# A TensorE that branches on each expert's token count, eleven more early casts, and a last norm shared by two engines

## The chip, the cores and the metric

The kernel is one launch on the 8 cores of a Trainium2 chip. Cores 0 to 3 are on one die, 4 to 7 on the other. No core waits for another, and each works on its own 1,024 tokens. The metric is the device time in microseconds of the slowest core.

## The reference

One transformer layer with the norms behind the residual sums. First attention over 4 sequences of 2,048 tokens (width 2,048, 16 causal heads of 128), then a norm; then a mixture of experts and another norm:

```python
h = relu(einsum('td,ndf->ntf', flat, shared_w1) + shared_b1)     # 2 shared experts, 1408 wide
out = flat + einsum('ntf,nfd->td', h, shared_w2) + shared_b2.sum(0)
scores = sigmoid(flat @ centroids.T) + bias                      # 16 routed experts
vals, idx = top_k(scores, 4)                                     # each token goes to 4 of them
gating = scattered vals / their sum
for each expert: rout += (relu(flat @ w1 + b1) @ w2 + b2) * g[:, None]
x = layernorm(x + out + rout)      # x is the input of this half
```

All inputs are float32; the kernel computes in bfloat16 with float32 sums. A core's 1,024 tokens times 4 choices over 16 experts make 256 tokens for an expert on average.

## The kernel before

**Stages.** Each core runs attention, then the output projection with the first norm (`wo_tile`, `ln1_tile`), then the router, then the 16 routed experts one after the other (the loop `for j in range(NR)`), and at the end the last group of the shared experts with the final norm (`dense_group(GROUPS[-1], ..., after_tile=final_norm)`).

**Two bodies.** After the router every engine reads a flag (L1254) and branches (L1255, L1257): the sparse body is run when no expert has more than CAP = 320 tokens, else a dense body that stands behind it in the instruction stream and is as long again.

**A routed expert (sparse body).** Its tokens are gathered by an indirect DMA (L1028) and turned by TensorE (`turn_batch`, L1043) into `xgT`, always 320 columns, with empty places where there are fewer tokens. The first product (L1127) takes 11 slices `fc` of 128 hidden units, 16 matmuls of 320 columns each; ScalarE applies the relu (L1134). The second product goes in two passes `h` over halves of the output: at each of 11 steps `fc`, four matmuls of 512 columns for the first two tiles of 128 tokens (L1154), and then two matmuls with 64 stationary columns (L1160) for the third tile, tokens 256 to 319. The results are written to `y_scr` by indirect DMAs (L1194). Between the steps `tick` spends a number of matmuls (`FILL_AT`) of the shared experts, which a generator hands out (L752, L774; DVE adds at L789).

**Weights.** They lie in HBM as float32 and are wanted as bfloat16 in units of 512 KB. A unit is either loaded by GpSimd's queue with a cast on the way (L687), or cast early from HBM to HBM into `wpre` by `precast` (L246) and later loaded as bfloat16 by SyncE's queue (L678). Experts 0, 2, 4, 6, 8, 10 and 14 (`PRE_EXPERTS`) are cast early, 22 units each; experts 1, 3, 5, 7, 9, 11, 12, 13 and 15 are cast at their load. The units go through a ring of 9 slots (two of them are held by the generator's group while it is open): `release` frees a slot when the last matmul that reads it is done, and `pump` then issues the next load in the order of use. The early casts are issued 6 after each load of attention's weights, `PRE_WO` = 16 after the loads of Wo, and the rest behind the loads of the first shared group. At most four are in flight (`DMA_POOLS["pre"]`), and GpSimd's queue waits in order.

**End.** `combine_load` and `combine_add` (L1091, L1096) add the experts' outputs. Then `final_norm` takes each of 8 token tiles: four bn_stats on VectorE (L572), a short chain of [128,1] operations (L580 to L586, with a Sqrt on ScalarE at L584), and two ScalarE passes that scale the tile (L807). VectorE's queue runs in program order, so the four additions of the next tile (L789) stand behind this tile's chain.

Of the kernel before, what the change touches and what calls it, by code (L numbers as in the profile page):

```python
# [15 lines left out]
D = 2048  # L16
# [6 lines left out]
FCH = 11  # L23
# [13 lines left out]
PRE_WO = 16  # L37
# [22 lines left out]
class SB:  # L60
# [50 lines left out]
    def mark(self, sem):  # L111
        return self.cnt.get(sem, 0)

# [21 lines left out]
def build_nc():  # L135
# [39 lines left out]
    sidx_sb = small("sidx_sb", 96, U32)  # L175
    flag_sb = small("flag_sb", 8, I32)
# [54 lines left out]
    sel_bf = carve(76800, 128)  # L231
    g_sb = carve(77056, 256, F32)
# [4 lines left out]
    def emit(plans):  # L237
# [353 lines left out]

        def wo_tile(n, ti, dns):
# [288 lines left out]
        flag_dv = sb.vchain(lambda e: e.tensor_scalar(flag_sb[:, 0:1], gsum[:, 8:9], CAP + 0.5, None, ALU.is_gt))  # L881
        sb.vchain(lambda e: e.tensor_scalar(pos, sel, -FAR, FAR - SHIFT, ALU.mult, ALU.add))
# [90 lines left out]
        IOA = bass.IndirectOffsetOnAxis  # L973
        limit_regs = {}
# [135 lines left out]
        for j in range(NR):  # L1110
# [29 lines left out]
            for h in range(2):  # L1140
# [7 lines left out]
                for fc in range(FCH):  # L1148
                    pu, po = divmod(h * FCH + fc, 2)
                    w = use(("w2", ge, pu))  # L1150
                    sb.wait("tensor", *hr_ready[fc])
                    for t in range(2):
                        for dn in range(2):
                            sb.mm((lambda e, fc=fc, w=w, po=po, t=t, dn=dn: e.matmul(  # L1154
                                psum_bank(2 * t + dn), Hr(fc)[:, t * 128:(t + 1) * 128],
                                w[:, po * 1024 + dn * 512: po * 1024 + (dn + 1) * 512],
                                start=(fc == 0), stop=(fc == FCH - 1), skip_group_check=True)), False)
                    end = fc == FCH - 1
                    for dn in range(2):
                        m = sb.mm((lambda e, fc=fc, w=w, po=po, dn=dn, end=end: e.matmul(  # L1160
                            PP[dn * 64:(dn + 1) * 64, 4 * 512:5 * 512], Hr(fc)[:, 256:CAP],
                            w[:, po * 1024 + dn * 512: po * 1024 + (dn + 1) * 512],
                            start=False, stop=end, skip_group_check=True)),
                            dn == 1 and (po == 1 or end))
                    if po == 1:
                        release(("w2", ge, pu), m)
                    if not end:
                        if j + 1 < NR and (h, fc) in TURN_AT:
                            turn_batch(j + 1, TURN_AT[h, fc])
                        tick(per)  # L1170
# [191 lines left out]
```

## Time and profile before

| | us |
|---|---|
| median of 3 runs (lowest, highest) | 2643.47 (2641.03, 2645.89) |
| the profiled execution, its own time | 2636.41 |
| its span on the slowest core (core 2) | 2634.7 |
| spans of the 8 cores | 2594.9 to 2634.7 |
| core 2: first matmul of expert 0 / of expert 15 / last matmul of expert 15 | 1258.1 / 2405.3 / about 2516 |
| PE busy, DMA share and granted clock over the span | 2296.7 (87%) / q0 73.9% and q1 15.6% / 0.945 |

The profiled execution's time is its span and 1.7 us around it, and lies 7 us below the median of the runs. A matmul's record is longer than the time until the next one can start, since they are pipelined, so rates are read from stretches of many. Rows name an engine, or its queue with a q behind it.

### The profile page before, as it was taken

The page shows a single profiled execution, that of the slowest core. Times are in us where ns is not written, and L with a number is a line of the kernel's source. Part 1 is how long each engine was busy: PE and PEld are TensorE (multiplying, and loading weights), DVE is VectorE, ACT ScalarE, POOL GpSimd, SP SyncE. Part 2 cuts the span into 40 slices and gives each one's busy share as a digit, 9 for nine tenths or more (in the row PEclk, how much of TensorE's full clock was granted, in tenths as well). Part 3 has the DMA queues.
Part 4 walks back from the last instruction along what each step waited for, and adds up shares of the span by engine and source line. Part 5 has one row for each costly group of instructions (what it writes and reads, how often), then busy time and mean ns, then how long its engine had stood idle before and what let it go on. Part 6 is the DMA issues. An engine that isn't in the chain of part 4 may idle for free.

```text
span 2634.7 us, 36044 instructions; the slowest of 8 cores (2594.9 to 2634.7 us)
## 1 busy us (share of the span) xinstructions
PE 2296.7 (87%) x13723; PEld 1200.7 (46%) x13723; DVE 865.8 (33%) x1397; ACT 544.2 (21%) x817; POOL 377.8 (14%) x583
## 2 busy tenths in 40 slices
PE   5879999999999569978989999899989988898776
PEld 3536646556466334423544444444534444244221
DVE  0234444444444334574201111113111031534356
ACT  0023333334334432201111111110101111011003
POOL 1001111111010000000021212122222212102100
PEclk9989999999999779999999999999999998999888
DMA  9499999999998895597499898989898999989973
GB/s 163 65 121 121 121 122 120 120 121 120 122 120 100 160 133 126 113 128 135 159 171 265 173 254 189 247 195 217 213 225 218 181 180 203 243 282 205 223 218 129
DMA packets 113360, 442.48 MB, mean 168 GB/s; under 512 B 16004, under 2 KB 16516, under 8 KB 103456
## 3 DMA queue, kind: packets, MB, share of 16 engines
q0 software_dynamic: 80208, 300.15, 73.9%
q1 hardware_dynamic: 32976, 139.94, 15.6%
q8 instruction: 116, 1.90, 0.3%
q14 instruction: 60, 0.49, 0.1%
HBM read 647.84 MB, written 139.46 MB: 299 GB/s over the span
## 4 chain that ended last, share of the span: by engine, by line
DMA 49%; PE 38%; DVE 6%; issue 4%; ACT 2%; POOL 1%; DVEq 0%; POOLq 0%; SPq 0%; ACTq 0%
DMA wpre<-w1x 12%; DMA wpre<-w2x 12%; DMA ar<-w2x 8%; PE PP L1154 8%; PE PP L1127 8%; DMA ar<-y_scr 6%; DMA ar<-w1x 5%; PE PP L774 4%; PE PP L598 3%; PE PP L1160 3%; PE PP L752 2%; PE PP L1043 2%; PE PP L322 2%; PE PP L341 2%; DVE ar L1096 1%
## 5 line engine op out<-in xcount | busy, mean ns | idle before, releaser
L1127 PE MATMUL PP<-ar 128*128 128x320 bf16 x2816 | 413.0, 305 | 44.0 <-DMA ar<-w1x 37.4
L1154 PE MATMUL PP<-ar 128*128 128x512 bf16 x1408 | 379.6, 394 | 17.5 <-DMA ar<-w2x 17.4
L1127 PEld LDWEIGHTS PP<-ar 128*128 128x128 bf16 x2816 | 276.4, 99 | 182.6 <-issue 64.2
L322 PE MATMUL PP<-ar 128*128 128x512 bf16 x1024 | 244.4, 382 | 29.4 <-DMA ar<-wqkv 29.3
L774 PE MATMUL PP<-ar 128*128 128x512 bf16 x704 | 208.4, 411 | 68.2 <-DVE ar L789 47.5
L477 ACT COPY ar<-PP 128x1024 bf16<-128x1024 bf16 (+1 forms) x192 | 153.3, 799 | 475.9 <-PE PP L466 475.9
L789 DVE SCALAR_TENSOR_TENSOR ar<-PP,ar 128x512 f32<-128x512 f32 x256 | 169.8, 688 | 218.8 <-PE PP L774 203.3
L341 PE MATMUL PP<-ar 128*128 128x256 bf16 x2048 | 241.5, 273 | 0.0
L1052 DVE COPY ar<-PP 128x960 bf16<-128x960 bf16 x96 | 55.9, 599 | 539.7 <-PE PP L1043 538.6
L436 DVE TENSOR_REDUCE st_sb<-PP 128x1 f32<-128x256 f32 (+7 forms) x128 | 173.7, 1357 | 171.7 <-PE PP L430 162.8
L341 PEld LDWEIGHTS PP<-ar 128*128 128x128 bf16 x2048 | 197.6, 98 | 30.3 <-issue 0.2
L1154 PEld LDWEIGHTS PP<-ar 128*128 128x128 bf16 x1408 | 124.7, 100 | 189.4 <-issue 76.9
L752 PE MATMUL PP<-ar 128*128 128x512 bf16 x704 | 174.0, 382 | 12.8 <-DVE ar L890 8.8
L1134 ACT ACTIVATE ar<-PP,b_sb 128x320 bf16<-128x320 f32 x176 | 92.8, 527 | 417.6 <-PE PP L1127 410.1
L306 PE MATMUL PP<-ar 128*128 128x512 bf16 (+1 forms) x576 | 130.5, 369 | 39.8 <-DMA ar<-xT 29.0
L1181 ACT COPY ar<-PP 128x512 f32<-128x512 f32 x64 | 34.4, 589 | 633.5 <-PE PP L1160 633.5
L322 PEld LDWEIGHTS PP<-ar 128*128 128x128 bf16 x1024 | 96.9, 98 | 134.2 <-issue 41.0
L446 ACT ACTIVATE ar<-PP,st_sb 128x256 bf16<-128x256 f32 (+7 forms) x128 | 156.9, 1226 | 0.5 <-DVE st_sb L436 0.5
L1160 PE MATMUL PP<-ar 128*64 128x512 bf16 x704 | 146.8, 414 | 0.0
L466 PE MATMUL PP<-cb_sb,ar 128*128 128x128 bf16 x1152 | 101.3, 227 | 37.5 <-ACT ar L477 32.5
L1096 DVE SCALAR_TENSOR_TENSOR ar<-ar,gk_sb 128x2048 f32<-128x2048 f32 x32 | 75.3, 2352 | 178.5 <-DMA ar<-y_scr 177.7
L687 POOL DMA_DIRECT2D ar<-w1x x117 | 65.1, 561 | 450.7 <-PE PP L1160 247.2
(117 smaller groups left out, 1858.7 us busy)
## 6 DMA issues: line engine op xcount, KB each, us to landing
ar<-wpre SPq DMA_DIRECT2D x162, 512.0 KB
ar<-w1x POOLq DMA_DIRECT2D x117, 512.0 KB, 14.1
ar<-w2x POOLq DMA_DIRECT2D x117, 512.0 KB, 19.1
wpre<-w1x POOLq DMA_DIRECT2D x81, 512.0 KB, 24.8
wpre<-w2x POOLq DMA_DIRECT2D x81, 512.0 KB, 24.8
ar<-y_scr SPq DMA_DIRECT2D x32, 1024.0 KB
ar<-wqkv POOLq DMA_DIRECT2D x24, 1024.0 KB, 25.1
ar<-xT POOLq DMA_DIRECT2D x8, 1024.0 KB, 27.1
```

The source lines that it names most:

```text
L306: (lambda e, dc=dc, rhs=rhs: e.matmul(ps[:, 0:w], w_at["q"][:, dc * 256 + jl * 128: dc * 256 + (jl + 1) * 128], rhs, start=(dc == 0), stop ...
L322: (lambda e, dc=dc: e.matmul(ps, w_at["k"][:, dc * 256 + jl * 128: dc * 256 + (jl + 1) * 128], x_bf[:, c * 8192 + dc * 512: c * 8192 + (dc ...
L341: (lambda e, dc=dc, tl=tl, sub=sub: e.matmul(ps[:, sub * 256:(sub + 1) * 256], x_bf[:, c * 8192 + dc * 512 + tl * 128: c * 8192 + dc * 512 ...
L436: sb.do("vector", lambda e: e.reduce_max(negmx_sp[up], PP[:, 0:kc], axis=AX.X, negate=True), "dv", 1)
L446: lambda e: e.activation(p_sb[up][:, 0:kc], PP[:, 0:kc], AF.Exp, bias=negmx_sp[up], scale=1.0, accum_out=lsum_sp[up]),
L477: lambda e: e.copy(dst, tb[:, 0:nbl * 128].rearrange("p (kb n) -> p kb n", n=128)), "ac", 1)
L752: m = sb.mm((lambda e, dc=dc, w=w, bank=bank, nt=nt: e.matmul(psum_bank(bank), w[:, dc * 128:(dc + 1) * 128], xhat[:, dc * 1024 + nt * 512 ...
L774: m = sb.mm((lambda e, j=j, w=w, bank=bank, ti=ti, dn=dn, last=last: e.matmul(psum_bank(bank), Hs[j][:, ti * 128:(ti + 1) * 128], w[:, dn ...
L789: x_mark[ti, dn] = sb.vec((lambda e, xs=xs, bank=bank, sc=sc: e.scalar_tensor_tensor(xs, psum_bank(bank), sc, xs, ALU.mult, ALU.add)))
L1127: m = sb.mm((lambda e, dc=dc, w=w, bank=bank: e.matmul(psum_bank(bank)[:, 0:CAP], w[:, dc * 128:(dc + 1) * 128], xgT[:, dc * CAP:(dc + 1) ...
L1154: sb.mm((lambda e, fc=fc, w=w, po=po, t=t, dn=dn: e.matmul(psum_bank(2 * t + dn), Hr(fc)[:, t * 128:(t + 1) * 128], w[:, po * 1024 + dn * ...
L1160: m = sb.mm((lambda e, fc=fc, w=w, po=po, dn=dn, end=end: e.matmul(PP[dn * 64:(dn + 1) * 64, 4 * 512:5 * 512], Hr(fc)[:, 256:CAP], w[:, po ...
```

## The change

Three edits. TensorE loads the 16 token counts into registers at the start of the sparse body. For each of the 11 slices of the first product it then has two versions of the 16 matmuls, one of 320 columns and one of 256, each under an If on the count. In the second product the third tile's matmuls are put ahead of the others, for two steps at a time (`PASS_STEPS`), under an If that leaves them out when the expert has at most 256 tokens. Eleven more units (the second product's weights of expert 12) are cast early, by `PRE_WO` = 27. In the final norm tiles 0, 2, 4 and 6 get their sums from two ScalarE passes with accumulation.

```diff
-PRE_WO = 16
+PRE_WO = 27
+PASS_STEPS = [[(0, 1), (2, 3), (4, 5), (6, 7), (8, 9), (10,)],
+              [(0,), (1, 2), (3, 4), (5, 6), (7, 8), (9, 10)]]
+PRE_HALF = 12
...
+    units += [("w2", 2 + PRE_HALF, u) for u in range(FCH)]
...
+        def act_scale(ti):
...
+            scr = final_scr
+            for dn in range(4):
+                sb.wait("scalar", *x_mark[ti, dn])
+            sb.act(lambda e: e.activation(scr, x_tm[ti], AF.Copy, bias=0.0, accum_out=ssum))
+            sb.wait("scalar", "ac")
+            m = sb.act(lambda e: e.activation(scr, x_tm[ti], AF.Square, accum_out=ssq))
+            sb.wait("vector", *m)
+            sb.vec(lambda e: e.tensor_scalar(mean, ssum, 1.0 / D, None, ALU.mult))
+            sb.vec(lambda e: e.tensor_scalar(r, ssq, 1.0 / D, EPS, ALU.mult, ALU.add))
+            sb.vchain(lambda e: e.scalar_tensor_tensor(bcol, mean, -1.0, mean, ALU.mult, ALU.mult))
+            sb.vchain(lambda e: e.tensor_tensor(r, r, bcol, ALU.add))
+            m = sb.vchain(lambda e: e.reciprocal(r, r))
...
         def final_norm(ti):
-            for chunk in range(4):
-                ln_stats(ti, chunk)
-            m, rinv, bcol, _, _ = ln_scale(ti, False)
+            if ti % 2:
+                for chunk in range(4):
+                    ln_stats(ti, chunk)
+                m, rinv, bcol, _, _ = ln_scale(ti, False)
+            else:
+                m, rinv, bcol = act_scale(ti)
...
+        cnt_dv = sb.vec(lambda e: e.tensor_scalar(cnt_sb[:, :], pbank[:, 128:144], 1.0, None, ALU.max))
...
+        sb.wait("tensor", *cnt_dv)
+        sb.take_counts("tensor")
...
-                for dc in range(16):
-                    sb.wait("tensor", *xgT_ready[j, dc // 3])
-                    m = sb.mm((lambda e, dc=dc, w=w, bank=bank: e.matmul(
-                        psum_bank(bank)[:, 0:CAP], w[:, dc * 128:(dc + 1) * 128], xgT[:, dc * CAP:(dc + 1) * CAP],
-                        start=(dc == 0), stop=(dc == 15), skip_group_check=True)), dc == 15)
+                for b in range(6):
+                    sb.wait("tensor", *xgT_ready[j, b])
+                m = sb.either("tensor", j, *[[(lambda e, dc=dc, w=w, bank=bank, cols=cols: e.matmul(
+                    psum_bank(bank)[:, 0:cols], w[:, dc * 128:(dc + 1) * 128], xgT[:, dc * CAP:dc * CAP + cols],
+                    start=(dc == 0), stop=(dc == 15), skip_group_check=True)) for dc in range(16)]
+                    for cols in (CAP, 256)])
...
-                for fc in range(FCH):
-                    pu, po = divmod(h * FCH + fc, 2)
+                for fcs in PASS_STEPS[h]:
+                    pu = (h * FCH + fcs[0]) // 2
                     w = use(("w2", ge, pu))
-                    sb.wait("tensor", *hr_ready[fc])
...
+                    for fc in fcs:
+                        sb.wait("tensor", *hr_ready[fc])
+                    sb.only_if("tensor", j, [(lambda e, fc=fc, w=w, po=(h * FCH + fc) % 2, dn=dn: e.matmul(
+                        PP[dn * 64:(dn + 1) * 64, 4 * 512:5 * 512], Hr(fc)[:, 256:CAP],
+                        w[:, po * 1024 + dn * 512: po * 1024 + (dn + 1) * 512],
+                        start=False, stop=(fc == FCH - 1), skip_group_check=True)) for fc in fcs for dn in range(2)])
...
+            if item[0] == "counts":
+                counts = [e.value_load(cnt_sb[0:1, i:i + 1]) for i in range(NR)]
+            elif item[0] == "if":
+                with e.If(counts[item[1]] > 256):
+                    for fn in item[2]:
+                        fn(e)
+            elif item[0] == "either":
+                with e.If(counts[item[1]] > 256):
+                    for fn in item[2][:-1]:
+                        fn(e)
+                    item[2][-1](e).then_inc(sems["pe"], 1)
+                with e.If(counts[item[1]] < 257):
+                    for fn in item[3][:-1]:
+                        fn(e)
+                    item[3][-1](e).then_inc(sems["pe"], 1)
```

The four L1154 matmuls of each step follow the If as before, and the slot is released behind them.

## Rows read from the trace of the kernel before

**Rows 1.** The cores: span from first to last instruction, mean granted clock.
```profile
core 0: 2632.3 us, clock 0.945
core 2: 2634.7 us, clock 0.945
core 7: 2630.7 us, clock 0.947
```

**Rows 2.** Core 2 by stretches, experts 0, 4, 5, 12: busy time (count), PEclk, DMA share, GB/s.
```profile
core 2: us, PE busy (x) PEld busy (x) DVE busy (x) ACT busy (x) POOL busy (x), PEclk, DMA share, GB/s
1258.00:1336.10 78.10, 76.91 (x433) 37.04 (x431) 18.46 (x28) 6.87 (x13) 12.16 (x15) 0.98 0.58 171
...
1559.30:1619.00 59.70, 59.70 (x361) 30.13 (x360) 7.12 (x12) 7.95 (x15) 12.38 (x15) 0.99 0.84 244
1619.00:1694.40 75.40, 62.77 (x360) 30.52 (x358) 7.12 (x12) 7.95 (x15) 17.55 (x25) 0.95 1.02 200
...
2109.10:2196.00 86.90, 78.12 (x425) 36.73 (x424) 29.10 (x44) 7.95 (x15) 21.69 (x33) 0.94 1.03 185
```

**Rows 3.** The same view inside expert 4, core 2.
```profile
1590.00:1595.00 5.00, 5.00 (x29) 1.91 (x28) 0.66 (x1) 0.00 (x0) 0.00 (x0) 1.00 0.49 120
```

**Rows 4.** Timeline of POOL, expert 4: start, duration, what [idle before].
```profile
1599.13 0.58 POOL L687 DMA_DIRECT2D ar<-w1x  x1 [32.99 <-PE PP L1160]
```

**Rows 5.** The chain that ended last, expert 2: start, duration, what.
```profile
1417.57 24.01 PE PP L1127 x176
```

**Rows 6.** Timeline of PE: 256-column matmuls; the last group's 512-column ones; two steps.
```profile
40.72 7.15 PE L341 MATMUL PP<-ar 128*128 128x256 bf16 x64
...
2516.49 27.80 PE L752 MATMUL PP<-ar 128*128 128x512 bf16 x128
...
1584.33 1.04 PE L1154 MATMUL PP<-ar 128*128 128x512 bf16 x4
1585.29 0.41 PE L1160 MATMUL PP<-ar 128*64 128x512 bf16 x2
1585.63 1.04 PE L1154 MATMUL PP<-ar 128*128 128x512 bf16 x4
```

**Rows 7.** TensorE's queue at the flag: register load and branches; ns min/median/max.
```profile
L1254 PEldq TENSOR_LOAD <-flag_sb x1: 485/485/485, 1203.4 to 1203.4; - x1
...
L1255 PEldq COMPARE_BRANCH  x2: 86/142/197, 1204.0 to 2618.2; - x2
...
L1257 PEldq COMPARE_BRANCH  x1: 3432/3432/3432, 2618.4 to 2618.4; - x1
```

**Rows 8.** Queues and issues in the stretch of expert 12, then of expert 4.
```profile
q0 software_dynamic: 4654, 16.01, 102.6%
...
q1 hardware_dynamic: 2519, 9.15, 44.1%
...
ar<-wpre SPq DMA_DIRECT2D x16, 512.0 KB
```

**Rows 9.** Timeline of POOL around the output projection, with one window of it.
```profile
1081.21 2.14 POOL L687 DMA_DIRECT2D ar<-w1x  x4 [81.68 <-PE PP L598]
...
1196.15 0.52 POOL L246 DMA_DIRECT2D wpre<-w2x  x1 [4.30 <-DMA wpre<-w2x]
1200.81 0.52 POOL L246 DMA_DIRECT2D wpre<-w2x  x1 [4.15 <-DMA wpre<-w2x]
...
1040.00:1060.00 20.00, 20.00 (x121) 9.77 (x119) 10.67 (x21) 4.28 (x3) 0.00 (x0) 1.00 0.07 27
```

**Rows 10.** The end: DVE's timeline of a tile, and groups with mean ns.
```profile
2573.00 3.09 DVE L572 BATCH_NORM_STATS2 ln_sb<-ar 128x6 f32<-128x512 f32 x4
...
2576.56 0.15 DVE L581 TENSOR_SCALAR ln_sb<-ln_sb 128x1 f32<-128x1 f32 x1
...
L446 ACT ACTIVATION_READ_ACCUMULATOR ar<-PP,st_sb 128x1 f32 x128 | 25.9, 202 | 0.0
...
L621 ACT ACTIVATE ar<-ar,ln_sb 128x2048 f32<-128x2048 f32 x8 | 16.6, 2080 | 0.0
```

More of the change, by code:

```diff
@@ L112, in mark, with take_counts, only_if, either @@
         return self.cnt.get(sem, 0)
+    def take_counts(self, eng):
+        self.ops[eng].append(("counts",))
+    def only_if(self, eng, expert, fns):
+        self.ops[eng].append(("if", expert, fns))
+    def either(self, eng, expert, fns, narrow_fns):
+        self.cnt["pe"] = self.cnt.get("pe", 0) + 1
+        self.ops[eng].append(("either", expert, fns, narrow_fns))
+        return ("pe", self.cnt["pe"])
     def vec(self, fn):
@@ L231, in build_nc @@
     sel_bf = carve(76800, 128)
+    final_scr = carve(69632, 4096, F32)
     g_sb = carve(77056, 256, F32)
@@ L590, in ln_scale @@
             return m, rinv, bcol, rinv2, bcol2
+        def act_scale(ti):
+            o = (ti % 2) * 32
+            ssum, ssq, mean, r = [ln_sb[:, o + i:o + i + 1] for i in range(4)]
+            rinv, bcol = ln_sb[:, o + 27:o + 28], ln_sb[:, o + 29:o + 30]
+            scr = final_scr
[10 more added lines that the diff above has]
+            m = sb.vchain(lambda e: e.reciprocal(r, r))
+            sb.wait("scalar", *m)
+            m = sb.act(lambda e: e.activation(rinv, r, AF.Sqrt))
+            sb.wait("vector", *m)
+            m = sb.vec(lambda e: e.scalar_tensor_tensor(bcol, mean, -1.0, rinv, ALU.mult, ALU.mult))
+            return m, rinv, bcol
         def wo_tile(n, ti, dns):
@@ L1147, in emit @@
                                          start=True, stop=False, skip_group_check=True), False)
-                for fc in range(FCH):
-                    pu, po = divmod(h * FCH + fc, 2)
+                for fcs in PASS_STEPS[h]:
+                    pu = (h * FCH + fcs[0]) // 2
                     w = use(("w2", ge, pu))
-                    sb.wait("tensor", *hr_ready[fc])
[L1152 to L1170, printed above, removed]
@@ new lines, in emit @@
+                    for fc in fcs:
[4 more added lines that the diff above has]
+                        start=False, stop=(fc == FCH - 1), skip_group_check=True)) for fc in fcs for dn in range(2)])
+                    for fc in fcs:
+                        po = (h * FCH + fc) % 2
+                        end = fc == FCH - 1
+                        for t in range(2):
+                            for dn in range(2):
+                                m = sb.mm((lambda e, fc=fc, w=w, po=po, t=t, dn=dn, end=end: e.matmul(
+                                    psum_bank(2 * t + dn), Hr(fc)[:, t * 128:(t + 1) * 128],
+                                    w[:, po * 1024 + dn * 512: po * 1024 + (dn + 1) * 512],
+                                    start=(fc == 0), stop=end, skip_group_check=True)),
+                                    t == 1 and dn == 1 and (po == 1 or end))
+                        if po == 1:
+                            release(("w2", ge, pu), m)
+                        if not end:
+                            if j + 1 < NR and (h, fc) in TURN_AT:
+                                turn_batch(j + 1, TURN_AT[h, fc])
+                            tick(per)
@@ L1239, in play @@
                 merged.append(item)
+        counts = []
         for item in merged:
-            if item[0] == "op":
+            if item[0] == "counts":
[13 more added lines that the diff above has]
+                    item[3][-1](e).then_inc(sems["pe"], 1)
+            elif item[0] == "op":
                 _, fn, sem, n = item
```

1 line of the change is left out of this document (added).

## The prediction, as put on record

> **What bounds the kernel now.** I read the spans of the cores first [rows 1]. Core 2 is the slowest and cores 0 and 7 stand within 4 us of it, so a gain counts only as far as all of them have it. Then I cut core 2 at the first L1127 matmul of each expert and read the stretches [rows 2]. The reader is to see two kinds. Expert 4, whose weights were cast early, takes 59.7 us, all of it PE busy, with the DMA engines at 0.84. Expert 5, whose weights are cast at their load, does the same matmuls in 75.4 us, PE busy 62.8 of it, with DMA at 1.02, which is full. Expert 12 (cast at its load, with 64 matmuls of shared work) is of the second kind: 86.9 us at 1.03. The other experts follow these two kinds (four of sixteen stretches stand in the rows). So TensorE sets the time in experts 2, 4, 6, 8 and 10, the transfers in the odd ones and in 12, 13 and 15. Expert 0 is TensorE's (0.58), and 14 nearly so.
>
> TensorE's savings are therefore worth something only while the DMA engines have idle time to give. In expert 4 that is 0.16 of 59.7, 9.6 us. It lies in the middle [rows 3]: the ring is full, and the first load for the next expert is issued at 1599.13, 39.8 us into the expert, when L1160 of the 11th step lets a slot go [rows 4]. From there to the end of expert 5 DMA is full. Whatever brings that load forward shortens the pair of experts.
>
> **Who is narrow.** The counts are in no row. I worked them out from the reference's router on the inputs of setup_inputs. Of 16 experts, 8, 7, 9, 8, 8, 8, 8 and 6 have at most 256 tokens on cores 0 to 7. Among the seven that are cast early these are, on core 0, experts 2, 8, 10; on core 2, experts 2, 4, 6, 10, 14; on core 7, experts 2, 4, 8, 10. (In the rows above expert 4 of core 2 has 254 tokens.)
>
> **First product, narrow.** 176 matmuls of 320 columns take 24.01 us [rows 5], 0.136 each. 64 of 256 columns take 7.15 us [rows 6], 0.112 each. 176 x 0.0247 = 4.3 us saved for a narrow expert, nothing for a wide one.
>
> **Third tile.** A step of the second product runs from 1584.33 to 1585.63, 1.30 us [rows 6]. Four of its matmuls have 512 columns at 27.80 / 128 = 0.217, together 0.87, so the two of L1160 cost 0.43. A narrow expert saves 22 x 0.43 = 9.5 us, and 4.7 of it lies in the first 11 steps, ahead of the load of [rows 4]. So that load comes 4.3 + 4.7 = 9.0 us earlier, and the idle DMA time of about 9.6 us can take it: I take 8.5 us for each narrow expert that was cast early. The bounds are 0 (the transfers slow down instead, see the rivals) and 14 (all of the saving). In a wide expert two steps' third tiles now stand together. The two L1160 of a step show 0.41 us busy where two in a row would take more, so they run side by side, and 0.43 is one slot of 0.217 and as much again for the change of shape. A pair of steps pays the change once: 0.21 us less, five pairs ahead of the load, 1.05 us a wide early-cast expert.
>
> In the experts that the transfers bound, a narrow one gains only behind its last unit, two steps, 0.9 us. Its L1127 and L1160 savings widen waits that are there already.
>
> **Eleven more units cast early.** In the stretch of expert 12 the cast queue takes 1.026 of 86.9 us, 89 us, for 24 units, the gathers and the scatters; with about 10 us for the latter it is 3.3 us a unit [rows 8]. In expert 4, 16 units from wpre take 0.441 of 60 us, 26.5 us, 1.5 to 1.65 each. So 11 x 1.8 = 20 us of DMA time leave expert 12. TensorE needs 59.7 + 64 x 0.217 = 73.6 us there when wide, so 13 us show at once and the rest goes to the loads of expert 13: I take 18 us, and 20 where expert 12 is narrow (core 0). The bounds are 13 and 22.
>
> The 11 casts themselves go into GpSimd's queue ahead of the first ring load, which today waits 81.68 us for a matmul of the output projection; a window of that time has DMA at 0.07 [rows 9]. Casts that have the engines alone follow each other at 4.66 us (1196.15 to 1200.81), 11 of them 51 us. With some 20 us taken off for what is still in flight, 60 of the 81.68 us are free. They fit, at no cost. If that cover were gone, they would cost 51 us. The number of casts left for later is 20 before and after.
>
> **Register loads.** A load of one register from SBUF takes TensorE's queue 0.485 us [rows 7]. Sixteen in a row are 7.8 us, at 1204, and expert 0 with its 0.58 of DMA can't take the delay up. I take 8 us, with the lost clock behind an idle stretch against what is still queued. The bounds are 3 (they overlap) and 9. What waits behind them is all of TensorE's sparse work, and with it the first slot that comes free.
>
> The Trainium skill (Runtime: NRT & Kernel Launch, "Instruction fetch mechanics") gives some 200 ns a register, in bulk too. By it the sixteen would be 3.2 us, an estimate from that page, and the time 4.6 us shorter. The trace's one load took 485 ns, and the sum goes by that.
>
> **Branches.** A slice of the first product gets three branch instructions (a skip, a compare that falls through, a jump at the end of the body), a group of steps one or two. The ones that went nowhere far took 86 and 197 ns [rows 7]; one slice has 0.3 to 0.6 us of them. TensorE's queue is a few matmuls ahead, and 16 matmuls give 1.8 to 2.2 us of cover. I take nothing. If the cover is gone, 0.2 us at each of 17 to 23 places in the 7 early-cast experts are 24 to 32 us.
>
> **Final norm.** A tile's four bn_stats and the aggregate keep VectorE 3.56 us (2573.00 to 2576.56) [rows 10]. On ScalarE a pass over 128x2048 takes 2.08 us and its accumulator 0.20, two of them 4.56 us, and VectorE's queue waits for them in order, ahead of the next tile's additions. Then come five short operations where there were two, 0.6 us more. So an even tile is 1.0 + 0.6 + 0.1 for the hand-over = 1.7 us longer, four of them 7 us, in a stretch where VectorE's chain sets the end. The last tile is odd and keeps its path. The bounds are 0 and 10. The dependent waits are TensorE's for banks, which only follow.
>
> **The sum.** Core 0: 3 x 8.5 + 4 x 1.05 + 20 + 5 x 0.9 = 54.2 us gained, 8 + 7 = 15 lost: 2632.3 - 39.2 = 2593.1. Core 2: 42.5 + 2.1 + 18 + 3.6 - 15 = 51.2: 2583.5. Core 7: 34 + 3.2 + 18 + 1.8 - 15 = 42.0: 2588.7. Core 0, with the fewest narrow experts among the early-cast, becomes the slowest, at 41.6 us less than core 2 had. The profiled execution took 2636.41, so 2594.8; the median of the runs stands at 2643.47, 7 us higher, and 41.6 less is 2602.
>
> **The rivals.**
> (A) *The transfers slow down instead.* If two cores that share the memory press on it with less idle time between, the cast loads get slower by what TensorE gives them, and the idle 9 us a pair are not to be had. For it: a unit of the same bytes costs the engines 3.3 us with a cast and 1.5 without [rows 8], so it is not the engines' own rate that a cast load goes by, and what limits it may be shared. Against it: in expert 4 the DMA engines idle with the ring full, not for lack of memory. Then 20 + 4 to 5 gained, 15 lost: -10, 2633.
> (B) *Far skips.* The branch over the dense body took 3.43 us [rows 7]. If a skip whose target is not at hand costs that much, and one in ten is such (my assumption, since the trace has one far skip alone), that is 27 of core 0's 11 x 16 + 12 x 8 = 272 skips, 27 x 3.43 = 93 us, about half in experts that TensorE bounds: 41 to 46 us, the whole gain. About 2643, no change.
> The Trainium skill (the same page and section) has the rule behind it: a taken branch whose target is outside the two fetched blocks of 256 instructions waits for a fetch. By that rule a skip of 33 into the next block is inside the window and pays nothing, so it speaks for the forecast; the row of 3.43 us, over a long body, agrees with the rule.
> (C) *Every taken skip pays the fetch.* Slower. 11 in each expert and 12 more in a narrow one. With 3.43 us each and about 1.2 us of cover, 2.2 us x 11 x 7 = 170 us in the early-cast experts, and in the others 24 us each against 10 to 15 us of waits, some 90 more; less the gain: about 2860. It decides from 41 / (7 x 17) = 0.35 us exposed at each place.
> (D) *The early casts run into the first ring loads*, because output projection and casts share memory: up to 51 us on the front, 2653, slower. Against it is the idle DMA in [rows 9].
> (E) *TensorE bounds more than I read*, and the cast experts give half of their savings too: on core 0 five narrow ones at 7 us, 35 in place of 4.5: about 2571. DMA at 1.02 and 1.03 speaks against it.
>
> **How the numbers follow.** Forecast 0.62, A 0.15, B 0.06, C 0.07, D 0.05, E 0.05. The median's own noise is about 0.2%, 5 us, which is what a measurement can tell from no change. Faster: forecast, A and E, less a little for A's lower edge, 0.80. Same: B and that edge, 0.08. Slower: C and D, 0.12. The range takes in A and B and, below, the upper bounds of the early-cast experts with cheap register loads and no loss at the end (39 + 5 + 7 + 8 gives about 2582, and 2575 with expert 12 at its bound): 2575 to 2642.
>
> **What would show it.** In the profile after: early-cast narrow experts at 50 to 52 us with DMA at 0.97 or more, and wide ones at 58 to 60; cast experts at DMA 1.02 as now; expert 12 near 70 us; a TensorE gap of about 8 us behind the flag; L246 issues in the place of the 81.68 us idle; even tiles of the last norm at 9.3 us, odd ones at 7.6. The prediction is wrong if L1127 of a wide expert takes visibly more than 24 us (branches exposed), if the cast experts grow by what the others lose (A), or if TensorE's queue shows branches of over 0.3 us.

## The result, and the profile after

| | before | after |
|---|---|---|
| median of 3 runs (lowest, highest), us | 2643.47 (2641.03, 2645.89) | 2627.20 (2625.21, 2628.79) |
| the profiled execution, its own time | 2636.41 | 2625.21 |
| mean of the 8 spans in it | 2615.4 | 2601.8 |

The ratio of after to before is 0.9938, 95% interval 0.9915 to 0.9961: a gain clear of the noise, but under 1%, 16.3 us at the medians where 41.5 were forecast. The time lies inside the stated range, and far from the forecast. (Some executions of every version, before's too, are disturbed by a lower clock of a whole die; ratios and counts of runs here leave them out.)

The spans of the cores, which answer to [rows 1]:
```profile
core 0: 2617.9 us, clock 0.931
...
core 2: 2612.0 us, clock 0.927
...
core 7: 2623.6 us, clock 0.928
```
Core 7 ends last. The granted clock is lower than before on all cores, and TensorE is busy for 84% of the slowest core's span, where it was 87%: matmuls went away, and most of their time didn't.

Core 2 by stretches, as in [rows 2]: experts 4, 5 and 12, and then the first product of expert 12 and the first pass of its second product (start:end, length, busy time and count of each engine, PEclk, DMA share, GB/s).
```profile
core 2: us, PE busy (x) PEld busy (x) DVE busy (x) ACT busy (x) POOL busy (x), PEclk, DMA share, GB/s
1560.70:1607.60 46.90, 46.37 (x311) 29.93 (x314) 7.10 (x12) 7.95 (x15) 11.55 (x14) 0.95 0.96 288
1607.60:1689.20 81.60, 63.39 (x356) 32.08 (x359) 7.10 (x12) 7.95 (x15) 18.50 (x27) 0.90 1.03 203
2078.90:2171.00 92.10, 77.30 (x413) 37.69 (x424) 27.65 (x42) 6.87 (x13) 16.02 (x22) 0.91 0.82 195
2078.90:2125.80 46.90, 33.44 (x194) 20.24 (x200) 7.97 (x12) 5.58 (x11) 6.30 (x9) 0.89 0.99 237
2125.80:2150.30 24.50, 23.27 (x133) 10.00 (x134) 11.79 (x18) 1.29 (x3) 2.07 (x3) 0.98 0.50 134
```
The reader is to see two things. Expert 4 went from 59.7 to 46.9 us and has its DMA engines at 0.96, so the idle time is used up. Expert 5 behind it grew from 75.4 to 81.6, and the pair gained 6.6 us. And expert 12, which was to fall to about 70 us, takes 92.1 with a DMA share of 0.82: transfers did leave it, and nothing came in their place.

Experts 4 and 12 on timelines of core 2 (PE, POOL, SyncE's queue, POOL), against [rows 4 to 6]:
```profile
1560.73 19.48 PE L1174 MATMUL PP<-ar 128*128 128x256 bf16 x171
...
1591.48 0.58 POOL L728 DMA_DIRECT2D ar<-w1x  x1 [24.49 <-PE PP L1210]
...
2104.36 36.11 SPq L719 DMA_DIRECT2D ar<-wpre  x11
...
2143.82 0.53 POOL L728 DMA_DIRECT2D ar<-w1x  x1 [41.11 <-PE PP L1210]
```
The narrow first product takes 19.5 us instead of 24.0, and the first load for expert 5 is issued 30.8 us into expert 4 instead of 39.8: earlier by just the 9.0 us that were worked out. The last two rows are expert 12. SyncE's queue issues its eleven units that were cast early from 2104.36 on, over 36.1 us, as slots come free. GpSimd, whose next cast load stands behind them in the order of use, issues nothing for 41.1 us, until 64.9 us into that expert.

TensorE's queue, against [rows 7] (count: ns min/median/max, first and last start):
```profile
L1293 PEldq TENSOR_LOAD <-cnt_sb x16: 296/302/320, 1208.7 to 1214.2; - x16
...
L1295 PEldq COMPARE_BRANCH  x276: 65/179/357, 1294.5 to 2486.0; - x138
...
L1299 PEldq COMPARE_BRANCH  x253: 65/176/655, 1265.3 to 2411.9; - x127
...
L1303 PEldq COMPARE_BRANCH  x275: 67/176/431, 1265.8 to 2412.2; - x138
```
None of these 804 branches of core 2 took more than 0.66 us. On the other cores eight of 5,700 took 0.8 to 1.8 us (more on them below).

The same cut, made on all eight cores and averaged, gives where the time went (us; "Wo" is from the first matmul of the output projection to the first of the shared experts, "start" from the flag to the first matmul of expert 0, "end" what follows expert 15's last matmul). The experiments of the next section stand in it too:

| | Wo | start | experts 0 to 11 | 12 | 13 | end | mean span |
|---|---|---|---|---|---|---|---|
| before | 122.3 | 50.6 | 835.1 | 85.5 | 118.1 | 120.9 | 2615.4 |
| after | 126.9 | 56.1 | 803.9 | 90.7 | 113.1 | 126.1 | 2601.8 |
| e1_branch | 120.6 | 56.6 | 803.7 | 89.5 | 120.4 | 120.9 | 2596.3 |
| e2_cast | 127.5 | 49.2 | 838.2 | 87.9 | 112.9 | 119.3 | 2618.0 |
| e4_w1 | 127.0 | 57.0 | 806.8 | 75.7 | 116.3 | 125.8 | 2593.7 |
| e6_lazy | 126.8 | 49.8 | 804.5 | 91.0 | 113.1 | 126.8 | 2597.5 |
| e13_w1_alone | 126.7 | 49.4 | 836.4 | 75.6 | 113.2 | 119.5 | 2602.9 |
| e12_later | 121.2 | 92.8 | 800.7 | 76.9 | 114.5 | 119.1 | 2605.6 |

Each row is one execution. They were taken on several chips, and the kernel before itself differs between them: its mean span is 2620.3 us over 19 counted runs beside e1 to e4, 2618.5 over 9 beside e6 to e9, and 2612.2 over 21 beside e10 to e13. The stretches can be compared across the rows, a few microseconds of the last column can't.

After against before: -31.2 in experts 0 to 11, and against it 4.6 + 5.5 + 5.2 in Wo, start and end, 0.2 in experts 12 and 13 together, and 1.8 in expert 15 (not in the table).

### The profile page after: what moved, and what is told of

The parts are those of the page before. It is cut to its first block, busy times and chain, and to the rows that moved or that the text cites. A ratio compares the mean times of both kernels' runs of the same rounds, so it can differ in the third digit from the quotient of the medians.

```text
span 2623.6 us, 36177 instructions; the slowest of 8 cores (2576.4 to 2623.6 us)
## 1 busy us (share of the span) xinstructions
PE 2201.3 (84%) x13371; PEld 1205.6 (46%) x13371; DVE 855.9 (33%) x1390; ACT 560.6 (21%) x833; POOL 378.0 (14%) x583
## 4 chain that ended last, share of the span: by engine, by line
DMA 46%; PE 40%; DVE 5%; issue 4%; ACT 3%; POOL 1%; DVEq 0%; POOLq 0%; ACTq 0%; SPq 0%
DMA wpre<-w2x 11%; DMA wpre<-w1x 10%; PE PP L1210 9%; DMA ar<-w2x 8%; PE PP L1174 7%; DMA ar<-w1x 6%; DMA ar<-y_scr 5%; PE PP L815 4%; PE PP L639 3%; PE PP L793 3%; PE PP L341 3%; PE PP L360 2%; PE PP L1090 2%; ACT ar L496 1%; DMA ar<-xT 1%
## 5 line engine op out<-in xcount | busy, mean ns | idle before, releaser
L1174 PE MATMUL PP<-ar 128*128 128x256 bf16 (+1 forms) x2816 | 385.9, 296 | 81.2 <-DMA ar<-w1x 64.6
L1174 PEld LDWEIGHTS PP<-ar 128*128 128x128 bf16 x2816 | 279.8, 101 | 196.3 <-issue 110.3
L1210 PEld LDWEIGHTS PP<-ar 128*128 128x128 bf16 x1408 | 132.3, 102 | 223.6 <-issue 106.6
L360 PEld LDWEIGHTS PP<-ar 128*128 128x128 bf16 x2048 | 197.7, 98 | 30.2 <-issue 0.2
L1182 ACT ACTIVATE ar<-PP,b_sb 128x320 bf16<-128x320 f32 x176 | 92.8, 527 | 424.9 <-PE PP L1174 424.9
L341 PEld LDWEIGHTS PP<-ar 128*128 128x128 bf16 x1024 | 97.2, 99 | 133.3 <-issue 40.2
L815 PEld LDWEIGHTS PP<-ar 128*128 128x128 bf16 x704 | 67.3, 104 | 184.5 <-issue 137.1
L1244 POOL DMA_INDIRECT y_scr<-ar,sidx_sb x96 | 96.3, 1003 | 215.3 <-DVE ar L1229 159.7
```

Of the source, the lines that this page charges most:

```text
L341: (lambda e, dc=dc: e.matmul(ps, w_at["k"][:, dc * 256 + jl * 128: dc * 256 + (jl + 1) * 128], x_bf[:, c * 8192 + dc * 512: c * 8192 + (dc ...
L360: (lambda e, dc=dc, tl=tl, sub=sub: e.matmul(ps[:, sub * 256:(sub + 1) * 256], x_bf[:, c * 8192 + dc * 512 + tl * 128: c * 8192 + dc * 512 ...
L815: m = sb.mm((lambda e, j=j, w=w, bank=bank, ti=ti, dn=dn, last=last: e.matmul(psum_bank(bank), Hs[j][:, ti * 128:(ti + 1) * 128], w[:, dn ...
L1174: m = sb.either("tensor", j, *[[(lambda e, dc=dc, w=w, bank=bank, cols=cols: e.matmul(psum_bank(bank)[:, 0:cols], w[:, dc * 128:(dc + 1) * ...
L1210: m = sb.mm((lambda e, fc=fc, w=w, po=po, t=t, dn=dn, end=end: e.matmul(psum_bank(2 * t + dn), Hr(fc)[:, t * 128:(t + 1) * 128], w[:, po * ...
```

## The experiments

Twelve kernels ran. The theory at the outset was that expert 12's early casts are worth nothing where they stand, since its first product still waits for loads with a cast; the rival was that cast loads as such had become slower (A of the prediction), or that branches and transfers share the loss.

**Each part alone.** e1_branch keeps only the branches, e2_cast only the casts, e3_norm only the norm. In e1:
```diff
-PRE_WO = 27
+PRE_WO = 16
-    units += [("w2", 2 + PRE_HALF, u) for u in range(FCH)]
...
-            if ti % 2:
-                for chunk in range(4):
-                    ln_stats(ti, chunk)
-                m, rinv, bcol, _, _ = ln_scale(ti, False)
-            else:
-                m, rinv, bcol = act_scale(ti)
+            for chunk in range(4):
+                ln_stats(ti, chunk)
+            m, rinv, bcol, _, _ = ln_scale(ti, False)
```
e2 takes that norm and the product loops of before, e3 the loops and casts of before.

> The branches and the new order alone (16 register loads, either, only_if), on the kernel before. Theory (the time was lost in the other edits and in expert 12): the early-cast narrow experts give 8 to 9 us a pair of experts as in the profile after, the register loads cost 6 to 7: on the slowest core 22 to 30 gained, about 2620. Rival (branches cost more than their gain on wide experts, or the transfers take it all back): within 5 us of 2643.

> The eleven early casts alone, on the kernel before. Prediction's step: 18 to 20 us gained, about 2624. Theory now: nothing of it shows, since the first product of expert 12 stays bound by its cast loads and the second by TensorE with the ring full; and 3 to 6 us are lost in the output projection, where a store of u waits behind the casts: 2643 to 2650. Expert 12 then has DMA idle time of 15 us or more in its second product. Rival: the casts are worth 18 us here too and only the combination with the branches hides it.

> The shared final norm alone, on the kernel before. Theory: VectorE waits in order for two ScalarE passes, an even tile gets 1.7 us longer, 7 us in all: 2650 (range 2647 to 2653). Rival (ScalarE relieves VectorE, the bound of the end): 4 x 3 us less, 2631.

Measured: e1 0.9917 (0.9884 to 0.9950), e2 1.0001 (0.9977 to 1.0026), e3 1.0013 (0.9999 to 1.0026). The three add up to -0.69%, the whole change measured -0.62%: no interaction is seen, with intervals of up to 0.3% either way. The branches are the gain, and eleven early casts are worth nothing. The norm is a small loss: its ratio's interval just reaches 0.9999, but the stretch at the end is 5.9 us longer, and the mean span of its counted runs is 5.3 us above before's. In e2 the casts took 5.2 us more in Wo and gave 5.2 back in expert 13; expert 12 itself grew by 2.4.

**The other half of expert 12 cast early.** e4_w1 changes one word of the changed kernel, and e13_w1_alone is e2 with the same word:
```diff
-    units += [("w2", 2 + PRE_HALF, u) for u in range(FCH)]
+    units += [("w1", 2 + PRE_HALF, u) for u in range(FCH)]
```


> The changed kernel with the first product's weights of expert 12 cast early in the place of the second's. Theory (in the changed kernel the slots come free too late to use the idle DMA time): now the ring fills fast in the first product and the casts of the second start early, so that about 15 us of the 18 show: 2609 to 2615. Rival (the DMA time saved is worth nothing, whichever half it is taken from, because TensorE bounds expert 12 as a whole): as the changed kernel, 2627 within 4 us.

> The kernel before with eleven more early casts as its only edit, but of expert 12's first product (e2_cast had the second product's and gave a ratio of 1.000). If what counts is which units are cast early, the stretch of expert 12 falls from 76 + 85.5 in (expert 11, 12) to about 70 in expert 12, experts 12 and 13 together by 15 to 18 us, against 5 us more in the output projection: mean 2603 to 2606, ratio 0.995 to 0.996. Rival: the gain was there only with TensorE's shorter experts, ratio 0.999 to 1.001.

Measured: e4 0.9893 (0.9871 to 0.9915), e13 0.9966 (0.9947 to 0.9985). Eleven units of the same size, cast at the same places in the queue, for the same expert: expert 12 takes 75.7 us in place of 90.7, and 75.6 in place of e2's 87.9. So the cost of a cast load was sized about rightly, and the place was wrong. Both came out somewhat short of what was expected: e4's counted runs have a median of 2621.4 us, above the 2609 to 2615, and in e13 experts 12 and 13 gave 14.8 us together, below the 15 to 18. (The intervals of e2 and e13 touch, so it is the stretch of expert 12 that tells the two apart.) Core 2 in e2_cast, the first product of expert 12 and the pass behind it:
```profile
2078.80:2120.20 41.40, 33.29 (x198) 20.30 (x200) 9.40 (x14) 6.63 (x13) 5.78 (x8) 0.88 0.98 208
2120.20:2145.90 25.70, 24.57 (x132) 9.91 (x133) 11.80 (x18) 1.33 (x3) 2.10 (x3) 0.97 0.48 128
```
and in e13_w1_alone, all of expert 12, and its first product:
```profile
2078.70:2154.20 75.50, 74.56 (x424) 36.28 (x422) 29.09 (x44) 7.95 (x15) 18.95 (x28) 0.98 0.98 201
2078.70:2108.00 29.30, 29.18 (x202) 19.35 (x200) 9.40 (x14) 6.65 (x13) 6.23 (x9) 1.00 0.97 231
```
The first product is 202 matmuls in both. It took 40.5 us before, 41.4 with the second half cast early, and 29.3, all busy, with the first half. Averaged over the cores it is 39.3 before, 41.7 in e2, 29.3 in e13. In e2 the pass behind it has the DMA engines at 0.48: the eleven cheap units have filled the ring, TensorE frees a slot only as fast as it multiplies, and the loads of expert 13 can't start. Over the cores 12.7 us of DMA time lie idle in that pass, 11.0 in the changed kernel, none before.

**Registers.** e6_lazy is the changed kernel with one load ahead of each expert in place of sixteen at the start:
```diff
+            sb.take_count("tensor", j)
...
-                counts = [e.value_load(cnt_sb[0:1, i:i + 1]) for i in range(NR)]
+                counts[item[1]] = e.value_load(cnt_sb[0:1, item[1]:item[1] + 1])
```


> The changed kernel with each expert's count loaded at the start of that expert, not all sixteen ahead of the first. Theory: the sixteen loads of 0.3 us in a row cost 5 to 6 us ahead of expert 0 and cost nothing when spread: the stretch from the flag to expert 0 is 6 us shorter, 2621. Rival (the delay is taken up later by the transfers): 2627.

Measured: 0.9888 (0.9851 to 0.9926), and the start is back at 49.8 us, from 56.1. (The interval overlaps that of the changed kernel; the 6.3 us are read from the stretch.) The sixteen loads are as many and as long as before, core 2:
```profile
L1293 PEldq TENSOR_LOAD <-cnt_sb x16: 298/308/497, 1253.9 to 2372.9; - x16
```
One at a time they are covered: no stretch is longer for them.

**The norm's chain put off.** e7_late issues an even tile's two sums at its place, and its chain and scaling only behind the four additions of the next tile, ahead of that tile's bn_stats:
```diff
+        sums = {}
         def final_norm(ti):
+            if ti % 2 == 0:
+                sums[ti] = act_sums(ti)
+                return
+            m, rinv, bcol = act_scale(ti - 1, sums[ti - 1])
+            final_out(ti - 1, m, rinv, bcol)
+            for chunk in range(4):
+                ln_stats(ti, chunk)
+            m, rinv, bcol, _, _ = ln_scale(ti, False)
+            final_out(ti, m, rinv, bcol)
```


> The changed kernel with the short chain of an even tile put behind the next tile's additions, so that VectorE no longer waits for ScalarE's passes. Theory (the loss at the end is VectorE's wait in order, not ScalarE's work): an even tile keeps VectorE some 4.2 us in the place of 7.6 before and 9.3 now, the stretch of the final norm is 4 x 5 = 20 us shorter than in the changed kernel, with TensorE's six matmul groups a tile as the next bound at 5.2 us: 2607 to 2614. Rival (ScalarE is the bound at the end): no change, 2627.

Only two of its runs count, 2624.16 and 2623.75 us, too few for a ratio; the stretch at the end took 125.1 us against 126.1. My theory fell. The wait that was to go is in the changed kernel's timeline, core 7:
```profile
2549.51 1.91 ACT L618 ACTIVATE ar<-ar 128x2048 f32<-128x2048 f32 x1 [21.41 <-DVE ar L830]
...
2551.61 1.91 ACT L620 ACTIVATE ar<-ar 128x2048 f32<-128x2048 f32 x1
...
2553.42 0.19 ACT L620 ACTIVATION_READ_ACCUMULATOR ar<-ar 128x1 f32 x1
...
2553.71 0.15 DVE L622 TENSOR_SCALAR ln_sb<-ln_sb 128x1 f32<-128x1 f32 x1 [4.29 <-ACT ar L620]
...
2570.45 0.15 DVE L622 TENSOR_SCALAR ln_sb<-ln_sb 128x1 f32<-128x1 f32 x1 [4.29 <-ACT ar L620]
```
and in e7_late that wait is gone, with others in its place:
```profile
2551.39 0.14 DVE L627 TENSOR_SCALAR ln_sb<-ln_sb 128x1 f32<-128x1 f32 x1
...
2558.38 1.86 PE L820 MATMUL PP<-ar 128*128 128x512 bf16 x4 [3.84 <-DVE ar L835]
...
2563.24 0.69 DVE L835 SCALAR_TENSOR_TENSOR ar<-PP,ar 128x512 f32<-128x512 f32 x1 [1.66 <-PE PP L826]
...
2569.36 0.14 DVE L627 TENSOR_SCALAR ln_sb<-ln_sb 128x1 f32<-128x1 f32 x1
```
A pair of tiles takes 18.0 us there against 16.7 in the changed kernel. The even tile's chain and the odd tile's bn_stats now follow each other on VectorE, TensorE stands 3.84 us without a bank, and runs on at the lower clock level: four matmuls of 512 columns take 1.86 us, where at the full 2.4 GHz they take 1.04 [rows 6]. Then VectorE waits 1.66 us for TensorE at each addition. The granted clock of such a pair is 0.72, against 0.80 in the changed kernel.

**How far narrowness carries.** Two changes of the constant in e1's Ifs. e8_allwide takes the 320 columns and the third tile always. e9_allnarrow never does, and so leaves out the tokens beyond the 256th of an expert; its time says what the experts would take if all were narrow:
```diff
# e8_allwide
-                with e.If(counts[item[1]] > 256):
+                with e.If(counts[item[1]] > 0):
...
-                with e.If(counts[item[1]] < 257):
+                with e.If(counts[item[1]] < 1):
# e9_allnarrow
-                with e.If(counts[item[1]] > 256):
+                with e.If(counts[item[1]] > 320):
...
-                with e.If(counts[item[1]] < 257):
+                with e.If(counts[item[1]] < 321):
```


> The branches alone on the kernel before, but with the threshold at 0: every expert runs the 320-column version and the third tile, through all the same branch instructions. It computes what the kernel before does. Theory (the branches are covered by TensorE's queue; the new order saves 2 us in an early-cast expert): 6 us for the register loads less some 7 us: 2641 to 2645, and an early-cast expert takes 57 to 58 us. Rival (branches are exposed at 0.2 us each place): early-cast experts of 62 us or more, 2660.

> The branches alone on the kernel before, but every expert runs the 256-column version and leaves the third tile out; tokens beyond the 256th of an expert are dropped, so this leaves out part of the computation. Theory (the savings are worth something only until the idle DMA time is used up): each early-cast expert gains 14 us of itself and a pair of experts 8 to 10, 6 pairs: mean of the cores' spans near 2580, 15 us under the branches alone, the slowest near 2600, with DMA full from expert 1 to expert 13. Rival (TensorE bounds the others too): 16 x 14 = 224 us less, 2430.

Measured: e8 0.9986 (0.9963 to 1.0009), e9 0.9846 (0.9809 to 0.9883). In e8 all branches are there and no matmul is saved. A first product on core 2:
```profile
1558.13 24.14 PE L1170 MATMUL PP<-ar 128*128 128x320 bf16 x170
```
That is the 24.01 of [rows 5]: the branches are covered. The early-cast experts 2 to 10 take 56.7 to 59.2 us, against 59.2 to 62.1 before, 2.3 to 3.7 less for the new order of the third tile, where 1.05 had been forecast. Two steps of the second product on core 2 in e8:
```profile
1583.33 0.62 PE L1197 MATMUL PP<-ar 128*64 128x512 bf16 x4
1583.89 1.90 PE L1206 MATMUL PP<-ar 128*128 128x512 bf16 x8
1585.72 0.62 PE L1197 MATMUL PP<-ar 128*64 128x512 bf16 x4
```
They take 2.39 us, where two single steps took 2.60 [rows 6]. That is the 0.21 us of the prediction, but an expert has ten such pairs, and all ten count and not only the five ahead of the load.

Averaged over the cores, experts 0 to 11 take 835.1 us before, 822.0 in e8, 803.7 in e1 and 791.5 in e9. So 13.1 of the 31.4 us between before and e1 come with the new order alone, and 18.3 with leaving work out in narrow experts. These are single executions. In the others this stretch stands at 835 to 841 us without branches and at 801 to 807 with them.

In e9, core 2, experts 4 and 5:
```profile
1533.30:1581.10 47.80, 46.48 (x315) 29.82 (x314) 7.11 (x12) 7.96 (x15) 11.53 (x14) 0.97 0.98 288
1581.10:1658.70 77.60, 52.41 (x316) 30.20 (x315) 7.11 (x12) 7.96 (x15) 18.51 (x27) 0.92 1.03 211
```
Expert 5 is narrow too, needs TensorE for 52.4 us, and takes 77.6. With every expert narrow the mean span is 2587.7 us, 8.6 below e1, where 15 had been expected. The first half of the experts gave 18.3 us in experts 0 to 11 and the second half 12.2. With the DMA engines at 0.98 and 1.03 the idle time is used up.

**Putting the better parts together.** e10_joined has e4's word, e6's registers and the old norm. e11_no_early is e1 with e6's registers and no early cast beyond those of before. e12_later is e10 with `PRE_WO = 16`, so that the eleven casts fall into the batch behind the first shared group.

> The changed kernel with three edits: the eleven units cast early are those of expert 12's first product, a count is loaded when its expert begins, and all tiles of the last norm take the old path. If the parts add: mean span of the eight cores 2593.7 (eleven units of the first product) less 6 to 7 for the register loads and less 5 for the norm, 2581 to 2583; ratio to the kernel before 0.984 to 0.986. Rival (the saved microseconds of the front are taken back, as the fetch of expert 0 and 1 is bound by the cast loads): mean above 2587, ratio 0.988 or more.

> The branches with the count loaded when its expert begins, and nothing else of the change. If the register loads cost the same 6 to 7 us here: mean span 2596.3 - 6.5 = 2590, ratio 0.989. Against e10_joined it shows what casting expert 12's first product early is worth when its cost in the output projection is counted: 18 us less in experts 12 and 13 against 5 to 6 us more before them, so 8 to 12 us for e10_joined. Rival: the two are equal within 3 us, and no early cast pays.

> As e10_joined, but only 16 units are cast ahead of the output projection, so eleven more are left for the queue behind the first shared group. If the early casts cost their 5 us because a store of u waits behind them, that stretch is back at 121 to 122 us, and expert 0 with its 28 us of idle DMA time takes the eleven: mean span 2576 to 2578. Rival: the loads of expert 1 are queued behind them (eleven at 4.66 us are 51 us), and experts 0 and 1 grow by 10 to 20 us: mean 2587 to 2597, slower than e10_joined.

Measured: e10 0.9913 (0.9877 to 0.9949), e11 0.9880 (0.9854 to 0.9906), e12 1.0000 (0.9985 to 1.0014). In e10 the mean span of the profiled execution came out as forecast, 2581.1, and the ratio didn't; e11 stands at 2580.3, 10 us under its forecast. Part of both is the chip, on which the kernel before has a mean span of 2612.2 us. Against that, the counted runs of e10 gained 32.6 us on the mean core, and those of e11 28.9. Over the counted runs, e10 (7) has a mean span of 2579.6 and a slowest core of 2610.2, e11 (4) 2583.3 and 2602.0. So e10 is ahead by 4 us on the average core, where 8 to 12 had been expected, and behind by 8 on the slowest, and the two intervals overlap: whether the early cast pays once the branches are there isn't settled. e11 is the shorter edit and no worse. Of the two only e11 has an interval (up to 0.9906) that is clear of the changed kernel's (from 0.9915).

e12 went against both of its expectations (its mean span is 2605.6 us). Wo is back at 121.2 us, as forecast, but the loss isn't in experts 0 and 1; it lies ahead of them. Core 2, POOL's timeline and one line of the waits (engine line <- what it waited for: us, times, longest):
```profile
1255.66 0.52 POOL L265 DMA_DIRECT2D wpre<-w1x  x1 [6.43 <-DMA wpre<-w1x]
1260.16 0.52 POOL L265 DMA_DIRECT2D wpre<-w1x  x1 [3.98 <-DMA wpre<-w1x]
1262.17 1.06 POOL L1071 DMA_INDIRECT ar<-u_scr,gidx_sb  x1 [1.50 <-issue]
```
```profile
PE PP L1086 <- DMA ar<-u_scr,gidx_sb: 42.4, 2, 41.0
```
The gather of expert 0's tokens stands in GpSimd's queue behind the casts, and TensorE waits 41.0 us for it. From the flag to expert 0 it takes 92.8 us, 43.0 more than e6_lazy. That is the price of eleven casts without cover, 3.9 us each; the prediction's 51 was of the right order.

## Why the prediction was right and wrong

**Right in the sum, by luck in part: the experts that TensorE bounded.** Core 0's experts 0 to 11 were to gain 25.5 + 3.2 = 28.7 us without the 0.9 of each narrow cast expert; they gained 28.5 (845.5 to 817.0). The mean over the cores is 31.2. The mechanism was as told (the load 9.0 us earlier, DMA share 0.84 to 0.96). Its two terms were both off, and cancel. By the branches' own trace 3.6 of the six early-cast experts 0 to 10 are narrow on the average core. At the prediction's prices the new order alone is worth 6 x 1.05 = 6.3 us and narrowness 3.6 x (8.5 - 1.05) = 27 us more; e8 and e1 have 13.1 and 18.3.

The bookkeeping differs too: a narrow expert gave more than 8.5 us (12.8 in expert 4 of core 2), and the cast expert behind it took some back (6.2 there). The prediction had named growing cast experts as a sign of rival A. They did grow, but A as a whole did not hold: the pairs gained. Its argument was weak as well: a load with a cast reads float32, so 3.3 us and 1.5 us were not for the same bytes read. Rival E (cast experts gain too) did not hold, e9 shows it at its plainest. Who is narrow was not quite right: the branches took the narrow version in 8, 7, 9, 9, 9, 8, 8 and 8 experts on cores 0 to 7, where the prediction has 8, 8 and 6 for cores 3, 4 and 7. Its early-cast ones on cores 0, 2 and 7 are right.

**Nearly right: branches at nothing.** The all-wide first product takes 24.14 us. Branches of over 0.3 us, which the prediction had named as a sign that it was wrong, are there, 579 of 6,504 on the eight cores, and nearly all are covered. A few are much longer and are not. On core 6 one of this line takes 1.82 us, at 1949.6, and TensorE idles behind it:
```profile
L1299 PEldq COMPARE_BRANCH  x264: 67/176/1823, 1260.6 to 2389.5; - x132
...
1944.77 5.41 PE L1174 MATMUL PP<-ar 128*128 128x256 bf16 x48
1951.62 1.92 PE L1174 MATMUL PP<-ar 128*128 128x256 bf16 x16 [1.44 <-issue]
```
There are at most three such on a core; what makes them long is not shown. The idle time put down to issue ahead of the experts' matmuls (gaps of over 0.15 us) is 4.8 us on the average core, 1.5 before. So some 3 us of the branches show, where 24 to 32 had been the price without cover. Rivals B and C, with 3.43 us a skip, are out. D held in small, by another way: no ring load was late, but the casts cost 5 us in Wo (below).

**Wrong: "So 11 x 1.8 = 20 us of DMA time leave expert 12", and "13 us show at once and the rest goes to the loads of expert 13: I take 18 us".** This is the step that failed. It treated the transfers of an expert as one sum. They are a sequence: the first product needs its eleven units first, those were still cast at their load, and a ring of nine slots (seven beside the generator's) can't pass what the later units save up to the earlier ones. So the first product stayed bound (46.9 us on core 2, 40.5 before), the cheap units behind it arrived ahead of need, and 11.0 us of DMA time ended idle. Experts 12 and 13 gave 6.1 us against e1_branch, where 18 to 20 had been taken. Against before they gave nothing, since the branches alone make them 6.3 us longer (85.5 + 118.1 to 89.5 + 120.4), a term that the prediction put at nothing. The same argument on the first half would have been about right: e4_w1 has 75.7 us, 15.0 less than the changed kernel, and experts 12 and 13 together 17.9 less than e1. That the first product even grew over before's is what e1 shows too, with no cast moved (46.6 us on core 2): it starts earlier than its loads can.

**Wrong in size: "They fit, at no cost".** The casts fit ahead of the first ring load, as forecast. On core 7 of the changed kernel:
```profile
1064.95 0.52 POOL L265 DMA_DIRECT2D wpre<-w2x  x1 [6.38 <-issue]
1084.05 2.14 POOL L728 DMA_DIRECT2D ar<-w1x  x4 [18.58 <-PE PP L639]
```
where before has 81.2 us of idle on this core, and 81.68 on core 2 [rows 9]. But it isn't the ring load that is late. It is a store of the first norm's output:
```profile
1022.09 2.09 ACT L656 ACTIVATE ar<-ar,ln_sb 128x2048 bf16<-128x2048 f32 x1 [7.22 <-DMA u_scr<-ar]
1024.33 1.87 PE L677 MATMUL PP<-cb_sb,ar 128*128 128x128 bf16 x16 [4.94 <-ACT ar L656]
```
ScalarE may write the next tile of u only when a buffer's store has landed, and TensorE turns that tile. TensorE's longest such wait is 1.0 to 2.9 us on the eight cores before, 3.7 to 6.3 after, and 0.3 to 1.8 with 16 casts (e12_later). The means are 1.8 and 4.8, so the wait accounts for 3.0 of the 4.6 us in Wo; the rest I didn't trace. I had looked for what is queued behind the casts on GpSimd, and not for what shares the DMA engines with them. Gain and cost cancel, and e2_cast is at 1.0001.

**Registers: 8 taken, 5.5 measured.** A load takes 302 ns in a row of sixteen, 4.8 us, and not the 485 of the flag's. The Trainium skill (Runtime: NRT & Kernel Launch, "Instruction fetch mechanics") has some 200 ns a register. By that the sixteen would be 3.2 us, an estimate from that page; the runs lie between the page and my row.

**Norm: 7 taken, 5.2 and 5.9 measured** (after, e3_norm). The passes took 1.91 + 0.18 and 1.91 + 0.19 us, VectorE waited 4.29 us for them, and even and odd tile together took 16.7 us, where the prediction had 9.3 + 7.6 = 16.9.

**Cores taken one at a time.** The prediction gave each core its own gain and took the slowest. The runs show that the two cores of a pair (0 and 1, 2 and 3, and so on) trade time (last section), so what counts is the pair's gain. Cores 0 and 1 have five narrow early-cast experts together, the other pairs ten, nine and seven, and in e1_branch the mean span of that pair fell by 17 us, of the others by 27, 22 and 22. So core 0 was read rightly as the laggard, but through its pair, and core 1 was never worked out.

Taken together, on the average core, by the prediction's own prices and the trace's narrow experts: 36 us for experts 0 to 11, 18 to 20 for expert 12's casts, 4 for experts 13 to 15, less 15, make about 43 us. The measured gain in the profiled executions is 13.6. Of the 29 to 30 us between them, some 19 are missing in experts 12 and 13, nearly 5 in experts 0 to 11, 4.6 in Wo, and some 5 in experts 14 and 15; registers and norm were 4.3 us too dear, which goes the other way. The slowest core follows the same terms, 41.5 against 16.3, but what the pairs shift from run to run lies on top, so I can't split its 25 us to the microsecond.

## What to carry to other kernels

Where a ring of buffers feeds an engine, a cheaper load is worth something only if it stands ahead of the wait; look which unit the first stall is for, and cheapen that one. A queue that has room is not proof that its work is free there: look also for the stores and loads of other queues that share the DMA engines in that time. Bring values for branches one at a time, where the engine's queue is ahead, and not all at the first use. And measure a change of order without the saving it comes with: here the order was 13 of 31 us.

## What the runs showed of the hardware

**Two cores of a pair trade time.** In 49 counted runs of the kernel before, on three chips, the spans of the two cores of a pair are 10 to 65 us apart, 32 to 35 on average, and either of the two can be the slower. Their correlation is -0.49 to -0.72, where between cores of different pairs it is never beyond 0.4 either way. (All runs are pooled; in the smallest set, nine runs on one chip, cores 0 and 1 rose and fell together.) Within one execution it is made in the cast experts: in the profiled one of before, experts 1, 3 and 7 take 81, 80 and 83 us on core 0 and 76, 75 and 75 on core 1, and the early-cast experts 2, 4, 6 and 8 are within 1.6 us of each other. It looks like transfers shared unevenly, which is not shown; nor does any run here show what decides which core gets more. The slowest of eight lies 23 us above the mean, so a mean over the cores tells two variants apart sooner than the device time does.

**A register load has two prices, and a row of them is not the reason.** The load of the flag takes 488 to 495 ns on every core of the changed kernel. The loads of the counts take 302 ns (median of core 2) sixteen in a row, and 308 in e6_lazy, where each stands alone, with single ones up to 648. What makes the flag's dearer is not shown.

**Idle costs twice.** The mean granted clock was 0.945 to 0.948 on the eight cores before and is 0.927 to 0.939 after. It goes with the matmuls left out and not with the branches: e8_allwide, with all branches and all matmuls, has 0.938 to 0.948, and e9_allnarrow, with the fewest, 0.920 to 0.929. In e7_late a stall of 3.84 us was followed by matmuls at 1.2 GHz (1.86 us for four, in place of 1.04).
